# Merging the semaphore signals of TensorE in the edge-attention loop of a graph network, and reordering its groups of matmuls

## What is computed

```
rad = relu(edge_attr @ W1 + b1) @ W2            # per edge, once for keys, once for values
g   = edge_sh @ Wang.T
k, v = (x[src] * g) @ Wlin * rad                # 64 and 128 columns
alpha = einsum(q[dst], Wdot, k)                 # 8 heads
attn  = softmax of alpha over the edges of one dst
out   = segment_sum(attn * v, dst) @ Wout
```

## Time and profile before

| What | Value |
|---|---|
| Median of 3 runs | 4296.25 us |
| The profiled execution: span from its first to its last instruction | 5039.6 us |
| The profiled execution's own time | not listed apart from its span |
| Ahead of the attention loop, in the profile | 1975 us |
| The attention loop, in the profile | 2941 us |
| Behind it, in the profile | 123 us |
| Granted TensorE clock in the loop | 0.91 of full |

### The profile page before, as it was taken

How to read it: one execution, slowest core, us unless ns; L and a number is a source line. 1 busy time by engine, 2 the same in 40 slices (tenths; PEclk the granted TensorE clock), 3 DMA queues, 4 the chain that set the end, 5 groups by cost and what they waited for, 6 DMA issues and landing times. The chain is left out here.

```text
span 5039.6 us, 74127 instructions
## 1 busy us (share of the span) xinstructions
PE 4108.6 (82%) x26543; PEld 3350.2 (66%) x26543; DVE 3024.4 (60%) x4129; ACT 1972.1 (39%) x2885; POOL 1919.0 (38%) x2002
## 2 busy tenths in 40 slices
PE   4667999999999984688888888888888888888832
PEld 4656999999999973465665666666666566666622
DVE  8985544544444342566666666666666666666734
ACT  5754666655665531222222223222223222222313
POOL 5640000000000015555555555555555555555352
PEclk9878999999999985799989999999999999999965
DMA  7998999999998533455555665556666655566433
GB/s 169 188 188 263 298 295 297 294 295 297 292 292 267 182 101 94 133 163 163 164 156 152 166 163 161 162 165 166 164 163 164 166 164 157 159 164 164 141 114 47
DMA packets 1012838, 944.08 MB, mean 187 GB/s; under 512 B 705677, under 2 KB 811929, under 8 KB 1012339
## 3 DMA queue, kind: packets, MB, share of 16 engines
q1 hardware_dynamic: 952099, 814.71, 55.7%
q0 software_dynamic: 60368, 124.52, 11.1%
HBM read 648.66 MB, written 289.97 MB: 186 GB/s over the span
## 5 line engine op out<-in xcount | busy, mean ns | idle before, releaser
L2313 POOL DMA_INDIRECT feats_hops<-x_table,src_s x1616 | 1546.9, 957 | 1223.1 <-PE e_turn_ps L2423 771.8
L1286 PE MATMUL acc<-t_wide,scaled 128*128 128x448 f32 x6860 | 1409.0, 366 | 24.2 <-DVE t_wide L1380 24.2
L1286 PEld LDWEIGHTS acc<-t_wide,scaled 128*128 128x128 f32 x6860 | 1284.3, 188 | 129.2 <-DVE scaled L1398 24.6
L1321 ACT CAST t_wide<-t_ring 128x1568 fp32r<-128x1568 uint8 x490 | 737.7, 1506 | 564.9 <-PE acc L1286 543.8
L1380 DVE CAST t_wide<-t_ring 128x1568 fp32r<-128x1568 uint8 x490 | 478.3, 976 | 733.4 <-PE acc L1286 714.9
L2484 ACT COPY e_out_rows<-e_turn_ps 128x512 f32<-128x512 f32 x404 | 222.1, 588 | 1026.5 <-remote 932.5
L1809 POOL MEMSET l_eps<- 128x1 f32 x1 | 0.1, 104 | 1452.9 <-POOLq L1498 1452.9
L2423 PE MATMUL e_turn_ps<-ident,feats_hops 128*128 128x128 f32 x1616 | 250.3, 296 | 355.6 <-ACT e_out_rows L2484 292.4
L2401 PE MATMUL e_ring_ps<-e_wlin_v,e_x_gv 128*128 128x128 f32 x3232 | 432.7, 281 | 96.9 <-issue 85.6
L2401 PEld LDWEIGHTS e_ring_ps<-e_wlin_v,e_x_gv 128*128 128x128 f32 x3232 | 393.0, 194 | 115.9 <-issue 102.2
L2569 DVE TENSOR_TENSOR e_lw<-e_ring_ps,e_w_t 128x1024 f32<-128x1024 f32 x202 | 247.1, 1223 | 366.9 <-remote 249.6
(11 more groups left out here) (272 smaller groups left out, 5096.2 us busy)
## 6 DMA issues: line engine op xcount, KB each, us to landing
t_ring<-adjacency_bytes SPq DMA_DIRECT2D x490, 512.0 KB, 5.8
sums_table<-e_out_rows SPq DMA_DIRECT2D x202, 576.0 KB
q_first<-hop_zeros_q SPq DMA_DIRECT2D x101, 512.0 KB, 5.9
e_sh<-parts_sh SPq DMA_DIRECT2D x404, 128.0 KB
e_ea<-parts_ea SPq DMA_DIRECT2D x404, 128.0 KB
e_q_rows<-q_first SPq DMA_DIRECT2D x404, 128.0 KB
e_same<-same_row SPq DMA_DIRECT2D x404, 128.0 KB
adjacency_bytes<-lists_staged SPq DMA_DIRECT2D x196, 256.0 KB
```

The costliest lines, as they stand in the source:

```text
L1286: mm = nc.tensor.matmul(acc[c][:, 0:n], U[p][:, b, :], wide[m % WIDE_RING][:, lo:lo + n], start=(b == 0 and p == 0), stop=(b == NB - 1 and ...
L1321: nc.scalar.copy(into, of).then_inc(wide_act, 1)
L2313: nc.gpsimd.indirect_dma_start(x_rows[i % XR][:, g * GT + t, :], None, x1_table, bass.IndirectOffsetOnAxis(ap=src_ix[:, at:at + 1], axis=0 ...
```

## The change

TensorE raises one semaphore per group. `p_xt`, `p_hid` and `p_seg` are raised once for two halves; `p_rk` goes into `p_lk`, as `p_keys`; `p_gk`, `p_gv`, `p_q` and (but for the last two iterations) `p_score` go into one `p_gates`, raised by the last gate matmul. `hidden` moves ahead of `scores`, `turn_q` ahead of the gates. By the `then_inc` calls that makes 7 raises per ordinary iteration where there were 14. All who waited for a merged signal wait for the later one.

```diff
@@ scores, keys, gates and the loop of TensorE
-                    mm.then_inc(p_seg, 1)
+                mm.then_inc(p_seg, 1)
...
             def scores(i):
...
-                mm.then_inc(p_score, 1)
+                if not on(i + 2):
+                    mm.then_inc(p_score, 1)
 
             def keys_and_radial(i):
...
-                nc.tensor.matmul(bank[:, 1, :], w2k[:], hid_k[s][:], start=True, stop=True).then_inc(p_rk, 1)
+                nc.tensor.matmul(bank[:, 1, :], w2k[:], hid_k[s][:], start=True, stop=True)
...
-                mm.then_inc(p_lk, 1)
+                mm.then_inc(p_keys, 1)
...
-                    tr.then_inc(p_xt, 1)
+                tr.then_inc(p_xt, 1)
...
-            def gates(r, n, done):
+            def gates(r):
                 s = r % 2
                 pe.wait_ge(sh_in[s], 32 * (r // 2 + 1))
-                bank = ring_bank(5 * r + n)
-                for g in range(2):
-                    mm = nc.tensor.matmul(bank[:, g, :], gate_w[:, 2 * n + g, :], sh[s][:], start=True, stop=True)
-                mm.then_inc(done, 1)
+                for n in range(2):
+                    bank = ring_bank(5 * r + n)
+                    for g in range(2):
+                        mm = nc.tensor.matmul(bank[:, g, :], gate_w[:, 2 * n + g, :], sh[s][:], start=True, stop=True)
+                mm.then_inc(p_gates, 1)
...
                 if on(i):
                     keys_and_radial(i)
+                if on(i + 1):
+                    hidden(i + 1, i)
                 if on(i - 1):
                     scores(i - 1)
                 if on(i + 1):
-                    hidden(i + 1, i)
-                    gates(i + 1, 0, p_gk)
-                    gates(i + 1, 1, p_gv)
                     turn_q(i + 1)
+                    gates(i + 1)
@@ who waits: new helper, SyncE, ScalarE, VectorE
+        def wait_scores(eng, k):
+
+            if k + 2 < N:
+                eng.wait_ge(p_gates, k + 3)
+            else:
+                eng.wait_ge(p_score, k + 3 - N)
...
-                    sp.wait_ge(p_gv, i - 1)
+                    sp.wait_ge(p_gates, i - 1)
...
-                if i >= 2:
-                    sp.wait_ge(p_q, i - 1)
...
+                act.wait_ge(p_seg, j + 1)
                 for h in range(2):
-                    act.wait_ge(p_seg, 2 * j + h + 1)
...
+                act.wait_ge(p_xt, r + 1)
                 for h in range(2):
-                    act.wait_ge(p_xt, 2 * r + h + 1)
...
-                act.wait_ge(p_hid, 2 * r + 1)
+                act.wait_ge(p_hid, r + 1)
                 if r >= 2:
-                    act.wait_ge(p_rk, r - 1)
+                    act.wait_ge(p_keys, r - 1)
...
-                dve.wait_ge(p_gk, i + 1)
+                dve.wait_ge(p_gates, i + 1)
...
-                dve.wait_ge(p_gv, i + 1)
...
-                dve.wait_ge(p_q, i + 1)
+                dve.wait_ge(p_gates, i + 1)
...
-                dve.wait_ge(p_rk, i + 1)
+                dve.wait_ge(p_keys, i + 1)
                 dve.wait_ge(v_q, i + 1)
...
-                dve.wait_ge(p_lk, i + 1)
                 dve.wait_ge(v_rkq, i + 1)
                 if i >= 2:
-                    dve.wait_ge(p_score, i - 1)
+                    wait_scores(dve, i - 2)
...
-                dve.wait_ge(p_score, scored_by(n))
+                wait_scores(dve, scored_by(n) - 1)
```

More of the change, by code:

```diff
@@ L2221, in edge_attention @@
         stored = sems("stored")
-        p_xt, p_gk, p_gv, p_hid, p_q = sem("p_xt"), sem("p_gk"), sem("p_gv"), sem("p_hid"), sem("p_q")
-        p_lk, p_rk, p_score = sem("p_lk"), sem("p_rk"), sem("p_score")
+        p_xt, p_hid, p_gates, p_keys, p_score = sem("p_xt"), sem("p_hid"), sem("p_gates"), sem("p_keys"), sem("p_score")
         p_lv, p_rv, p_seg, p_wt = sem("p_lv"), sem("p_rv"), sem("p_seg"), sem("p_wt")
@@ L2258, in load @@
                 if i >= 2:
-                    sp.wait_ge(p_hid, 2 * (i - 1))
+                    sp.wait_ge(p_hid, i - 1)
                 for g in range(2):
@@ L2308, in _ @@
                 if i >= XR:
-                    pool.wait_ge(p_xt, 2 * (i - XR + 1))
+                    pool.wait_ge(p_xt, i - XR + 1)
                 for g in range(2):
@@ L2433, in hidden @@
                         pe.wait_ge(a_wt, 3 * chain_at(i - 2) + 2 + n)
-                    nc.tensor.matmul(turn_ps[:, n, :], stack[:, n * D:(n + 1) * D], ea[s][:],
-                                     start=True, stop=True).then_inc(p_hid, 1)
+                    mm = nc.tensor.matmul(turn_ps[:, n, :], stack[:, n * D:(n + 1) * D], ea[s][:],
+                                          start=True, stop=True)
+                mm.then_inc(p_hid, 1)
             def turn_q(r):
@@ L2442, in turn_q @@
                 for t in range(GT):
-                    tr = nc.tensor.transpose(q_ps[:, t * P:(t + 1) * P], q_rows[s][:, t, :, :].rearrange("p g q -> p (g q)"), ident[:])
-                tr.then_inc(p_q, 1)
-            def gates(r, n, done):
+                    nc.tensor.transpose(q_ps[:, t * P:(t + 1) * P], q_rows[s][:, t, :, :].rearrange("p g q -> p (g q)"), ident[:])
+            def gates(r):
                 s = r % 2
                 pe.wait_ge(sh_in[s], 32 * (r // 2 + 1))
-                bank = ring_bank(5 * r + n)
-                for g in range(2):
-                    mm = nc.tensor.matmul(bank[:, g, :], gate_w[:, 2 * n + g, :], sh[s][:], start=True, stop=True)
-                mm.then_inc(done, 1)
+                for n in range(2):
[3 more added lines that the diff above has]
+                mm.then_inc(p_gates, 1)
             for i in ITERATIONS:
@@ L2553, in find_spots @@
             def find_spots(i, j):
-                dve.wait_ge(p_score, min(i - 1, N))
+                wait_scores(dve, min(i - 2, N - 1))
                 nc.vector.tensor_copy(score_ps[:, 2 * P:2 * P + K], fpos[:, j * K:(j + 1) * K]).then_inc(v_spot, 1)
                 if j >= 2:
-                    dve.wait_ge(p_seg, 2 * (j - 1))
+                    dve.wait_ge(p_seg, j - 1)
                 dve.wait_ge(v_spot, 2 * j + 1)
```

3 lines of the change are left out of this document (1 added, 2 removed).

## The result

The changed kernel takes **4429.07 us** (median of 4 runs, 4425.35 to 4430.85), the kernel before, on the same chip, 4296.77 us (4296.08 to 4298.28). The ratio is 1.0303, with a 95% interval of 1.0291 to 1.0316: slower by 132 us. The time lies in the forecast range, 4290 to 4445 us. The size was not hit: 83 us were forecast, 132 measured.

The account below looks back on a forecast made before the run. TensorE was taken to bound the loop, at 10.21 of 10.88 us per iteration. The terms 80 - 12 + 15 = +83 us on the runs' 4296 gave 4379 us, range 4290 to 4445.

Parts of the forecast that it names:

- TensorE sets the pace, and the 743 us belong to one profiled execution: Attention loop: TensorE needs 10.21 of 10.88 us per iteration; the profile's 743 us over the runs is mostly its own lateness.
- the 136 us: Runs' loop of 2198 us less TensorE's need: the most left for late signals, part of it filling and draining.
- A raise costs nothing: TensorE's stream: seven raises fewer gain 0.00, since spread_out and values both take 1.95 us.
- find_most waits for the gates: +80 us: VectorE's first scan starts 1.85 us later, delaying `gate`; `values` on TensorE then idle 1.60 us, 50 times.
- keep_x: +15 us: keep_x's copies wait for both halves of turn_x, so turn_weights start 0.29 us later, 50 times.
- The order gives 12 us back: In the add_weights iteration the gates' second pair no longer waits 0.23 us for `prod`, 50 times: -12 us.
- gate, keep_hidden, keep_rows and rkq covered: These waits for merged signals cost 0, hidden behind other TensorE work; for rkq and prod the cover is 0.02 us.
- faster: Rival: late signals are in the runs too, and half as many raises are late by less: 4265 us, chance 0.18.
- no change: Rival: new waits fall where TensorE waits already, or GpSimd's 10.0 us lets stalls be caught up: 4296 us, chance 0.08.
- The clock rival: Much slower: each new 1.60 us stall brings TensorE to half clock, 129 us on top: 4508 us, chance 0.08.

Follow-up runs that it names:

- score_apart: The changed kernel with `p_score` raised in each iteration and waited for by find_most, find_spots and prod, 8 raises: 4356.97 us.
- more_raises: The kernel before with 20 more raises per iteration on a semaphore that nobody waits for: 4297.58 us, ratio 1.0001.
- xt_apart: The changed kernel with `p_xt` raised for each half again and keep_x waiting for each half: 4409.21 us.
- sums_later: The kernel before with add_weights moved behind keys on VectorE, nothing else: 4272.53 us, ratio 0.9941.
- halves_merged: The kernel before with `p_seg` and `p_hid` merged as in the change, nothing else: 4298.65 us against 4298.66.
- signals_only: The changed kernel in the old order of groups (scores, hidden, gates, turn_q), with `p_gates` raised by turn_q: 4428.16 us, ratio 1.0299.
- order_only: The kernel before with the new order alone (hidden, scores, turn_q, gates), all 14 raises kept: 4335.42 us against 4297.89.
- hidden_first: The kernel before with hidden ahead of scores and nothing else moved (hidden, scores, gates, turn_q): 4355.89 us, ratio 1.0132.

## Why the prediction was right, and where it fell short

- **TensorE sets the pace, and the 743 us belong to one profiled execution.** Right: the profiles of all 13 other executions agree with their runs. The loop is about 2140 us, not 2198, since the stretch took in a piece of the last layer; so the 136 us that the prediction left open for waits and lateness were about 80.
- **A raise costs nothing.** Right, from two rows of 1.95 us; shown with 4040 raises more, at most 1.1 ns each.
- **find_most waits for the gates: +80 us.** Right in place, chain and count; 1.31 us of idle time for 1.60 worked out, and 72 us by score_apart. The step costs 1.47 us start to start. In the undisturbed profile of `more_raises` the same place before the change is:

```profile
3020.00 1.08 PE L2396 MATMUL e_ring_ps<-feats_hops,e_wlin_k 128*64 128x512 f32 x4
...
3021.91 0.68 DVE L2620 TENSOR_TENSOR_SCAN e_top<-e_neg,e_score_ps 128x256 f32<-128x256 f32 x1
...
3023.69 1.21 DVE L2553 TENSOR_TENSOR feats_hops<-e_ring_ps,e_x_t 128x1024 f32<-128x1024 f32 x1
...
3025.15 1.95 PE L2404 MATMUL e_ring_ps<-e_wlin_v,e_x_gv 128*128 128x128 f32 x16
```

  The scan starts 1.91 us after keys, where the working had 1.74 from the disturbed profile, so the added wait was sized 0.17 too large; the cover, 3025.15 - 3024.90 less the hand-over of 0.05, was 0.20, not 0.25. The 0.31 us of slower steps delay the scan and the values alike.
- **keep_x: +15 us.** 20 us by xt_apart: turn_weights start 0.40 us later, for 0.29 worked out.
- **The order gives 12 us back.** The wait is 25 us in the runs (sums_later). It was read in the disturbed profile, where VectorE's `prod` ended 2.49 us after the start of keys; in the undisturbed ones it ends 2.79 after, and the wait is 0.54 us, not 0.23.
- **gate, keep_hidden, keep_rows and rkq covered.** Right for the change: no such wait in its list, and halves_merged is the kernel before to 0.01 us. The working had `rkq` right at 1.13 us after keys, but took 1.02 from it to `prod`, with a gap of 0.33 that was a wait for keys and is gone: it takes 0.73, `prod` ends at 2.55 and the cover is larger than the 0.02 worked out. Only in the old order, where the gates stand some 0.65 us earlier, does it cost, 34 us by signals_only. (In the working of `gate` the tail is 1.10 - 0.94 = 0.16 us, not 0.17; the 5.16 there goes with 0.16.)
- **The step that failed:** each group of TensorE was given the duration that it had next to its old neighbours, "the new order of TensorE is hidden, scores, turn_q, gates" with the old steps of 0.91, 0.56, 0.53, 0.44. The cost of moving a group was put at nothing, without a reason. It is +63 us by the steps; order_only shows 37.5 net of what comes back, and hidden_first 57 for the swap of hidden and scores alone.

The sum by runs: the order 37.5 (63 less what comes back), find_most 72, keep_x 20, together 130 of the 132 us. The forecast put 83 because it left out the 63 and sized the give-back 13 too small, with find_most 8 too large and keep_x 5 too small. Of the rivals, "faster" and "no change" fell with the result, and more_raises and score_apart show why: the number of raises costs nothing, and the stall behind find_most is not caught up. The clock rival fell too: in the stretch that it came from the earlier trace rows, 3506.3 to 3512 us, the granted clock was 0.53; in the loop of the changed kernel it is 0.98, and values take 2.05 us behind a stall where they take 1.95 elsewhere. That the 37.5, 72 and 20 add is a property of this order; by signals_only the old order has other terms with the same total.

## What to carry to other kernels

Here a raise on TensorE's stream cost at most 1.1 ns, and a late raise up to 72 us over the loop: merge signals only where you can name what covers the waiting engine, in the order that you will ship, since moving one group takes the cover of another. Before reordering groups of matmuls, ask who their new neighbours are; here TensorE lost 0.31 us per iteration between groups without one idle gap in the list of waits, so compare starts to starts. Know which iteration you are reading: one in four had a wait of its own before the change, and a merged signal adds nothing there. And set a profile's span beside the runs before reading any of its waits: here the profile of before invited a cure for a delay that the runs don't have.

## What the runs showed that was not expected

One profiled execution of 14, that of the kernel before, ran 743 us over its runs, with waits that the profile could put to no instruction. That TensorE's signals were taken up late is how the prediction reads these rows; it was not shown. The 13 others, with 7 to 34 raises per iteration, agree with their runs to a few us. What made that one late is open; the kernel before was not profiled a second time.

Neighbours cost TensorE time: with a 128\*128 group between two 128\*64 groups, 0.10 us more behind keys, 0.10 behind hidden, 0.05 behind scores, and 0.12 behind gates when they follow scores, 0.37 us per iteration. Over the loop the swap alone costs 57 us, after what the gates no longer wait.
